# A head loop's turn re-ordered in 48 places, with the next group's first key products in its last eight, and a buffer of its own for the spread blocks' sum

## The chip, the cores and the metric

The kernel runs on one core of a Trainium2 chip. Its time is the device time of one execution in microseconds (us). Five engines work side by side, each through its own list of instructions in order: TensorE (PE, with its weight loads as PEld), VectorE (DVE), ScalarE (ACT), GpSimd (POOL) and SyncE (SP), which here only issues DMAs. They hand work to each other by semaphores.

## What is computed

The reference is a layer norm, followed by a gated delta-rule attention and a mixture of 16 experts on a part of the tokens, both added to the input. The part that this case is about, cut to what matters:

```python
q = silu(causal_dwconv(x @ Wq)); k = silu(causal_dwconv(x @ Wk)) * DK**-0.5; v = silu(causal_dwconv(x @ Wv))
alpha = sigmoid(x @ Wa + ba); beta = sigmoid(x @ Wb + bb)
def step(S, inps):
    qt, kt, vt, at, bt = inps
    Sk = einsum('bhvk,bhk->bhv', S, kt)
    err = Sk - vt
    S = at * S - bt * (err[..., None] * kt[:, :, None, :])
    ot = einsum('bhvk,bhk->bhv', S, qt)
    return S, ot
o = layernorm(scan(step)) * sigmoid(x @ Wg)      # per head
out = x + o @ Wo + experts(x)
```

There are 2 batches of 2048 tokens, 16 heads of width 128, and a model width of 512. All of it is float32; a projection is made as three fp32r products (high times high, high times low, low times high).

## The kernel before

Three stages follow each other: `prepare` (layer norm, experts, gates), `heads` (projections, convolution and scan for each head) and `project` (the output product). The change touches `heads` alone.

`heads` works on 32 batch-heads (`NH`), each in four groups of 512 tokens (g = 0 to 3), each group in four chunks of 128 tokens. One call of `turn` is one group's time step of a software pipeline. In the same turn an engine does work for groups at several ages:

- **Projection.** 48 products (12 for key, 12 query, 12 value, 12 gate; `project_some`) of the group that is four turns ahead of the scan, into three PSUM banks that take turns (`PJ_OF`). A bank is used again when its last reader has freed it (`PJ_FREED`): a convolution on DVE (`CONV_AT`, three multiply-adds for each of key, query and value) or the gate's tanh on ACT.
- **Inverse.** The scan over 128 tokens is solved with the inverse of a triangular matrix. PE makes the products `kT kT` (L_AT), DVE multiplies them into `LT` (LT_AT), ACT copies their diagonal blocks (DIAG_AT), POOL masks and sums them (LC_AT), SP stores the sum in DRAM twice and loads it back spread over all partitions as `Lb` (`spread`), POOL solves blocks of 16 in 15 steps of two instructions (`SOLVE_AT`), writes them back (T16P_AT), DVE transposes them into `Tnb` (T16_AT), and PE builds the larger blocks in two visits (`VISIT_AT`: visit 0 and visit 1).
- **The chain.** Twelve steps (`CHAIN`), three for each chunk, carry the state `S` on: k = 0, 3, 6, 9 is `S kT` on PE, answered by `R` on DVE; k = 1, 4, 7, 10 is `R TT` on PE, answered by `Wc` on ACT; k = 2, 5, 8, 11 is `Wc k_rows` on PE, answered by `S` on DVE.
- **Output.** The group's output is normalised by four DVE instructions `on` (ON_AT, one for each chunk), turned on PE (ON_TURN_AT), scaled on ACT (OT_AT) and gated on POOL (`oG`, OG_AT).
- **Weights of the next head.** Each of the four is cut once per head into a high part on ACT and a low part `w_lo` on POOL (`CUT_AT`: three in a turn with g = 3 and one in the next with g = 0).

The order on every engine is written out by hand: a turn has `STEPS` places, and each item's `_AT` number says in which place it stands. The number orders only instructions of one engine; nothing holds two engines at the same place. Before, there are 38 places, and PE sends its 48 products in one or two pieces at each.

Short names below: a "piece" is one of the 48 products, "V0" and "V1" are the visits, "k6" is chain step 6, "place 25" is s = 25.

```python
def wait(eng, sem, value):
    if isinstance(value, int) and value <= 0:
        return
    eng.wait_ge(sem, value)
```

Of the kernel before, what the change touches and what calls it, by code (L numbers as in the profile page):

```python
# [734 lines left out]
def heads(nc, bank, ident, pow_half, xT_hi_d, xT_lo_d, gates_d, base_d, oT_d, x_hi, x_lo, w_raw, w_cut, weights, taps, ln_w, ln_b,  # L735
# [10 lines left out]
    with ExitStack() as ctx:  # L746
# [760 lines left out]
        def _(pe):  # L1507
            def turn(pe, hh, g, n, chain, late, mid, inv, proj, ln, tile=None):
                at = counter(hh, g)
                par, cur = (g + 1) % 2, g % 2  # L1510
                sent = [0]

                def bank_waits(i):

                    back, user = PJ_FREED[g][i]
                    if user == 3:
                        wait(pe, tanh_done, at(1, 5 - back))
                    else:
                        wait(pe, conv_done, at(9, 4 - back, 3 * user + 3))
# [362 lines left out]
```

## Time and profile before

| | |
|---|---|
| median of three runs | 3578.73 us (3572.82 to 3580.15) |
| the profiled execution | 3573.76 us, its span 3568.4 us |
| PE busy | 3490.3 us, 98% of the span |
| DVE, ACT, POOL busy | 68%, 65%, 54% |
| granted TensorE clock, mean | 0.995 of full speed |
| stage `heads` | from about 418 us to about 3277 us of the span |
| first and last `LT` on DVE, one in each of 128 turns | 429.7 us and 3154.0 us |

PE's busy share is of little use by itself, since matmuls overlap: a piece is recorded with about 0.4 us but the next one starts 0.23 us after it. What a thing costs on PE is the distance from its start to the start of the next.

### The profile page before, as it was taken

The numbers are of one execution on the slowest core, as the hardware profiler recorded it, in microseconds if no ns is written. First come the engines' busy times: TensorE is split into PE (matmuls) and PEld (weight loads), VectorE is DVE, ScalarE is ACT, GpSimd is POOL, SyncE is SP. The second block draws the span as 40 slices with busy tenths as digits, with TensorE's granted clock in tenths as the row PEclk, the third lists the DMA queues.
The fourth block names the chain that finished last, engine by engine and source line by source line (L and its number), as shares of the span: only waits on it lengthen the run. The fifth ranks groups of instructions, "written<-read, shape, count | busy, mean of one in ns | idle before, by whom it ended". The sixth has DMA issues, their size and how long they took to land. (4 is left out here: it accounts for less than half of the span.)

```text
span 3568.4 us, 105534 instructions
## 1 busy us (share of the span) xinstructions
PE 3490.3 (98%) x32308; PEld 2912.9 (82%) x32308; DVE 2419.8 (68%) x5785; ACT 2303.3 (65%) x6448; POOL 1913.2 (54%) x4905
## 2 busy tenths in 40 slices
PE   8999989999999999999999999999999999999999
PEld 6787768888888888888888888888888888877887
DVE  6656557777777777777777777777777777753222
ACT  4443357777777777777777777777777777752111
POOL 3323256666666666666666666666666666653000
PEclk9999999999999999999999999999999999999999
DMA  8654523333333333333533333333333333444453
GB/s 307 217 197 164 172 60 76 77 83 87 82 79 77 77 81 82 77 79 76 146 102 84 79 77 78 76 77 85 79 76 79 76 77 81 107 156 127 142 148 111
DMA packets 427681, 375.89 MB, mean 105 GB/s; under 512 B 191984, under 2 KB 323056, under 8 KB 421248
## 3 DMA queue, kind: packets, MB, share of 16 engines
q1 hardware_dynamic: 424000, 362.46, 37.1%
q0 software_dynamic: 2080, 6.82, 0.5%
q8 instruction: 261, 4.28, 0.5%
q14 instruction: 284, 2.33, 0.2%
q10 hardware_dynamic: 1056, 0.02, 0.0%
HBM read 292.62 MB, written 76.58 MB: 103 GB/s over the span
## 5 line engine op out<-in xcount | busy, mean ns | idle before, releaser
L1329 DVE SCALAR_TENSOR_TENSOR conv<-bank,tap,conv 128x512 f32<-128x512 f32 x1152 | 862.3, 749 | 152.1 <-ACT conv L1465 123.9
L1155 POOL TENSOR_TENSOR prods<-Lb,Tc 128x60 f32<-128x60 f32 (+14 forms) x1920 | 480.1, 250 | 604.2 <-DMA Lb<-base_d 460.3
L1535 PE MATMUL bank<-hx_hi,w_hi 128*128 128x512 f32 x1536 | 664.3, 433 | 0.0
L1535 PE MATMUL bank<-hx_hi,w_lo 128*128 128x512 f32 x1536 | 645.3, 420 | 14.3 <-DVE Tnb L1291 11.5
L1535 PE MATMUL bank<-hx_lo,w_hi 128*128 128x512 f32 x1536 | 638.4, 416 | 0.0
L1162 POOL TENSOR_TENSOR Tc<-Tc,prods 128x56 f32<-128x56 f32 (+13 forms) x1792 | 460.1, 257 | 141.2 <-POOL prods L1155 1.7
L1446 ACT ACTIVATE Wc<-bank 128x128 f32<-128x128 f32 x512 | 140.9, 275 | 371.0 <-PE bank L1637 330.6
L1535 PEld LDWEIGHTS bank<-hx_hi,w_lo 128*128 128x128 f32 x1536 | 293.2, 191 | 50.9 <-DVE Tnb L1291 17.1
L1283 DVE SCALAR_TENSOR_TENSOR S<-S,gamma,bank 128x128 f32<-128x128 f32 x480 | 166.9, 348 | 234.3 <-PE bank L1648 221.0
L1535 PEld LDWEIGHTS bank<-hx_hi,w_hi 128*128 128x128 f32 x1536 | 292.4, 190 | 36.5
L1535 PEld LDWEIGHTS bank<-hx_lo,w_hi 128*128 128x128 f32 x1536 | 292.7, 191 | 29.5
L1465 ACT ACTIVATE conv<-bank,tap 128x512 f32<-128x512 f32 x384 | 264.4, 688 | 12.5
L1270 DVE SCALAR_TENSOR_TENSOR R<-bank,scale_c,v_rows 128x128 f32<-128x128 f32 x480 | 166.6, 347 | 125.4 <-PE bank L1624 125.4
L1637 PEld LDWEIGHTS bank<-R,TT 128*128 128x128 f32 x960 | 170.6, 188 | 85.3 <-DVE R L1270 39.4
L1139 POOL TENSOR_TENSOR w_lo<-w_raw,w_hi 128x512 fp32r<-128x512 f32 x152 | 194.9, 1283 | 74.1 <-ACT w_hi L1359 74.1
L1535 PE MATMUL bank<-x_hi,w_lo 128*128 128x512 f32 x512 | 212.0, 414 | 12.5 <-DVE Tnb L1291 8.1
L1535 PE MATMUL bank<-x_hi,w_hi 128*128 128x512 f32 x512 | 221.3, 432 | 1.0 <-PEq L151 1.0
L1648 PEld LDWEIGHTS bank<-Wc,k_rows 128*128 128x128 f32 x960 | 170.9, 189 | 60.8 <-ACT Wc L1446 35.8
L1624 PEld LDWEIGHTS bank<-S,kT 128*128 128x128 f32 x960 | 180.8, 189 | 41.8 <-DVE S L1283 0.7
L1535 PE MATMUL bank<-x_lo,w_hi 128*128 128x512 f32 x512 | 212.9, 416 | 0.0
L1397 ACT ACTIVATE same<-LT 32x128 f32<-32x128 f32 x512 | 157.1, 307 | 85.7 <-DVE LT L1348 72.7
L1648 PE MATMUL bank<-Wc,k_rows 128*128 128x128 f32 x960 | 197.4, 287 | 4.1
(211 smaller groups left out, 8855.4 us busy)
## 6 DMA issues: line engine op xcount, KB each, us to landing
Lb<-base_d SPq DMA_DIRECT2D x128, 512.0 KB, 4.7
gamma<-gamma_d SPq DMA_DIRECT2D x128, 258.0 KB, 3.5
alpha<-alpha_d SPq DMA_DIRECT2D x128, 256.0 KB, 3.2
oT_d<-oG SPq DMA_DIRECT2D x128, 256.0 KB, 4.4
gu_raw<-in_gate_up SPq DMA_DIRECT2D x16, 1408.0 KB, 6.3
o_raw<-oT_d SPq DMA_DIRECT2D x13, 1024.0 KB, 6.9
w_raw<-oT_d SPq DMA_DIRECT2D x12, 1024.0 KB, 7.0
dn_raw<-in_down SPq DMA_DIRECT2D x44, 256.0 KB, 6.7
```

The lines of the kernel that those rows point to most:

```text
L1139: pool.tensor_tensor(w_lo[:, i], w_raw[:, i], w_hi[:, i].bitcast(F32), ALU.subtract).then_inc(wlo_done, 1)
L1155: pool.tensor_tensor(prods[:, :, i + 1:], Lb[:, i, :, i + 1:], Tc[:, :, i:i + 1].to_broadcast([P, G, SB - 1 - i]), ALU.mult)\
L1162: pool.tensor_tensor(Tc[:, :, i + 1:], (sel if i == 0 else Tc)[:, :, i + 1:], prods[:, :, i + 1:], ALU.subtract).then_inc(solve_done, 1)
L1270: dve.scalar_tensor_tensor(out=R[:], in0=CO[:, 0:D], scalar=scale[:, cur, c:c + 1], in1=v_rows[:, cur, c], op0=ALU.mult, op1=ALU.add)\
L1283: dve.scalar_tensor_tensor(out=S[:], in0=S[:], scalar=gamma[:, cur, c, C:C + 1], in1=CO[:, 2 * D:3 * D], op0=ALU.mult, op1=ALU.add)\
L1329: dve.scalar_tensor_tensor(out=conv[i][:, to], in0=PJ[PJ_OF[g][i]][:], scalar=tap[:, i, j + 1:j + 2], in1=conv[i][:, to], op0=ALU.mult, op ...
L1397: act.activation(diag[quad(q)], LT[quad(q), g, :, quad(q)], ACT.Copy).then_inc(diag_done, 1)
L1465: act.activation(conv[i][:, KS - 1:], PJ[PJ_OF[g][i]][:], ACT.Copy, scale=tap[:, i, 0:1])\
L1535: last = pe.matmul(dst, a[:, i, k], b[:, k], start=(j == 0), stop=(j == 3 * KC - 1))
L1624: pe.matmul(CO[:, 0:D], kT[:, n % 6, chunk(c)], S[:], start=True, stop=True).then_inc(chain_done, 1)
L1637: pe.matmul(CO[:, D:2 * D], TT[:, n % 3, c], R[:], start=True, stop=True)\
L1648: pe.matmul(CO[:, 2 * D:3 * D], k_rows[:, cur, c], Wc[:], start=True, stop=True)\
```

## The change

The tables get new numbers for a turn of 48 places with exactly one piece in each. `LEAD = 8` shifts the pieces against the turn: a turn begins with piece 8 of its own group, and its last eight places take the first eight key pieces of the next group. The very first turn sends eight pieces ahead of its first place; the turns that make output tiles follow suit. `Lc`, the sum that SP stores, gets a buffer of its own instead of sharing `prods` with the solve, and the waits that guarded the shared one are changed; to make room, `Tn64` becomes the unused half of `MT`.

```diff
-STEPS = 38
+STEPS = 48
+LEAD = 8
-CHAIN = {0: 0, 7: 1, 8: 2, 11: 3, 15: 4, 18: 5, 19: 6, 22: 7, 23: 8, 26: 9, 28: 10, 36: 11}
+CHAIN = {0: 0, 6: 1, 9: 2, 14: 3, 18: 4, 20: 5, 22: 6, 25: 7, 27: 8, 33: 9, 40: 10, 43: 11}
-CUT_AT = {(3, 13): 0, (3, 21): 1, (3, 28): 2, (0, 19): 3}
+CUT_AT = {(3, 21): 0, (3, 30): 1, (3, 33): 2, (0, 14): 3}
...
-        Lc = prods
+        Lc = sb("Lc", [P, G, SB])
...
-        Tn64 = sb("Tn64", [2 * TB, G, 2 * TB])
+        Tn64 = MT[0:2 * TB]
...
-                sp.wait_ge(base_stored, at(32, d + 1))
+                stored = fixed(sp, at(32, d + 1), NH * GROUPS * 32)
+                solved = fixed(sp, at(SOLVE_PER, d), NH * GROUPS * SOLVE_PER)
+                sp.wait_ge(base_stored, stored)
+                wait(sp, solve_done, solved)
...
-                        wait(pool, solve_done, at(SOLVE_PER, 4))
+                        wait(pool, base_stored, at(32, 4))
...
-                        wait(act, masked, at(1, 4))
+                        wait(act, lc_done, at(1, 4))
...
-                sent = [0]
+                sent = [LEAD if proj and not (isinstance(hh, int) and hh < 0 and g == 0) or tile == 0 else 0]
...
+                        ahead, piece = divmod(sent[0], 3 * KC * NPROJ)
+                        i, j = divmod(piece, 3 * KC)
...
+                        hp, gp = (hh, g + ahead) if g + ahead < GROUPS else (hh + 1, 0)
+                        dst = PJ[PJ_OF[gp][i]][:]
...
+                if proj and isinstance(hh, int) and hh < 0 and g == 0:
+                    project_some(LEAD)
```

Other table entries that the prediction speaks of, before and after: L_AT 18 and 21, V0 20 and 33, V1 1 and 0, T16_AT 18 and 26, LT_AT 18 and 25, ON_AT 20 and 33, ON_TURN_AT 22 and 40, YB_AT 31 and 45, QG_AT (`q_gamma`) 24 and 22, OG_AT 25 and 34.

DVE, in the turn (0, 3) ahead of the loop, from the second chain `S` to the normalisation of the output. Before (the lines shown are numbered as in the kernel before):

```order
L1283 SCALAR_TENSOR_TENSOR S<-S,gamma,bank6 128x128 [waits s_done,chain_done]
L1291 STREAM_TRANSPOSE Tnb<-TTb 128x128 [waits tn_placed,mid_done,t16_done]
L1348 SCALAR_TENSOR_TENSOR LT<-bank5,decay 128x512 [waits late_done,diag_done,decay_done,l_done]
L1270 SCALAR_TENSOR_TENSOR R<-bank6,scale_c,v_rows 128x128 [waits chain_done]
L1315 TENSOR_SCALAR on<-o,hmv,hrstd 128x128 [waits o_turned,hrstd_done]
L1315 TENSOR_SCALAR on<-o,hmv,hrstd 128x128 x3
```

The same stretch of DVE's list after (lines from here on are three to five higher than before):

```order
L1286 SCALAR_TENSOR_TENSOR S<-S,gamma,bank6 128x128 [waits s_done,chain_done]
L1332 SCALAR_TENSOR_TENSOR conv1<-bank1,tap,conv1 128x512 [waits tap_done]
L1273 SCALAR_TENSOR_TENSOR R<-bank6,scale_c,v_rows 128x128 [waits chain_done]
L1332 SCALAR_TENSOR_TENSOR conv1<-bank1,tap,conv1 128x512 [waits conv_done]
L1351 SCALAR_TENSOR_TENSOR LT<-bank5,decay 128x512 [waits late_done,diag_done,decay_done,l_done]
L1294 STREAM_TRANSPOSE Tnb<-TTb 128x128 [waits tn_placed,mid_done,t16_done]
L1332 SCALAR_TENSOR_TENSOR conv1<-bank1,tap,conv1 128x512 [waits conv_done]
L1286 SCALAR_TENSOR_TENSOR S<-S,gamma,bank6 128x128 [waits s_done,chain_done]
L1273 SCALAR_TENSOR_TENSOR R<-bank6,scale_c,v_rows 128x128 [waits chain_done]
L1318 TENSOR_SCALAR on<-o,hmv,hrstd 128x128 [waits o_turned,hrstd_done]
L1318 TENSOR_SCALAR on<-o,hmv,hrstd 128x128 x3
```

`Tnb` of the last solve stood ahead of `LT` and stands behind it now; three convolutions of the query stand between the chain's answers.

POOL in a turn with g = 3, from the end of the solve on. Before:

```order
L1177 TENSOR_TENSOR TTb<-Tc,same_c 128x128 [waits placed,mid_done,solve_done]
L1183 TENSOR_TENSOR hrstd<-hveps,pow_half 128x4 [waits hveps_done]
L1139 TENSOR_TENSOR w_lo<-w_raw,w_hi 128x512 [waits whi_done]
L1167 TENSOR_TENSOR same<-same,same_c 128x128 [waits diag_done]
L1171 TENSOR_TENSOR prods<-same 128x64 [waits masked,solve_done]
L1139 TENSOR_TENSOR w_lo<-w_raw,w_hi 128x512 [waits whi_done]
L1189 TENSOR_TENSOR q_gamma<-qT,gamma 128x512 [waits chain_done,gamma_loaded0,silu_done]
L1197 TENSOR_TENSOR oG<-oT,gT 128x512 [waits gate_done,o_stored,oT_done]
L1139 TENSOR_TENSOR w_lo<-w_raw,w_hi 128x512 [waits whi_done]
```

After:

```order
L1180 TENSOR_TENSOR TTb<-Tc,same_c 128x128 [waits placed,mid_done,solve_done]
L1186 TENSOR_TENSOR hrstd<-hveps,pow_half 128x4 [waits hveps_done]
L1170 TENSOR_TENSOR same<-same,same_c 128x128 [waits diag_done]
L1174 TENSOR_TENSOR Lc<-same 128x64 [waits masked,base_stored]
L1142 TENSOR_TENSOR w_lo<-w_raw,w_hi 128x512 [waits whi_done]
L1192 TENSOR_TENSOR q_gamma<-qT,gamma 128x512 [waits chain_done,gamma_loaded0,silu_done]
L1142 TENSOR_TENSOR w_lo<-w_raw,w_hi 128x512 [waits whi_done] x2
```

The three weight cuts of the turn now stand all behind the sum, `q_gamma` between the first and the second, with nothing else in between; `oG` follows them.

PE in the loop, g = 1, from the products of `LT` to V0. Before (REGISTER_ALU rows are waits and counts of the sequencer):

```order
L1702 MATMUL bank5<-kT 128x128 x4
L1535 MATMUL bank0<-hx_hi1,w_hi 128x512
L1535 MATMUL bank0<-hx_lo1,w_hi 128x512
L1623 REGISTER_ALU
L1624 MATMUL bank6<-S,kT 128x128
L1562 REGISTER_ALU
L1566 REGISTER_ALU
L1535 MATMUL bank0<-hx_hi1,w_lo 128x512
L1589 MATMUL bank3<-Tnb,LT 32x32 x16
```

After, the end of the same way for g = 2:

```order
L1653 MATMUL bank6<-Wc,k_rows 128x128
L1659 MATMUL bank7<-Wc,AT 128x128
L87 REGISTER_ALU
L1540 MATMUL bank2<-hx_hi2,w_hi 128x512
L1540 MATMUL bank2<-hx_lo2,w_hi 128x512
L1540 MATMUL bank2<-hx_hi2,w_lo 128x512
L1540 MATMUL bank2<-hx_hi2,w_hi 128x512
L1540 MATMUL bank2<-hx_lo2,w_hi 128x512
L1567 REGISTER_ALU
L1571 REGISTER_ALU
L1540 MATMUL bank2<-hx_hi2,w_lo 128x512
L1594 MATMUL bank3<-Tnb,LT 32x32 x16
```

Between the products of `LT` and V0 stood three pieces and one chain matmul; now twelve pieces and five chain matmuls stand there, of which the last six pieces and two matmuls are shown.

## Rows read from the trace of the kernel before

**Rows 1.** The page: busy time of each engine, and its costliest DVE group.

```profile
PE 3490.3 (98%) x32308; PEld 2912.9 (82%) x32308; DVE 2419.8 (68%) x5785; ACT 2303.3 (65%) x6448; POOL 1913.2 (54%) x4905
...
L1329 DVE SCALAR_TENSOR_TENSOR conv<-bank,tap,conv 128x512 f32<-128x512 f32 x1152 | 862.3, 749 | 152.1 <-ACT conv L1465 123.9
```

**Rows 2.** Line L1348, one in each turn: count, durations, first and last start.

```profile
L1348 DVE SCALAR_TENSOR_TENSOR LT<-bank,decay x128: 652/685/694, 429.7 to 3154.0; 128x512 f32<-128x512 f32 x128
```

**Rows 3.** Timeline of PE, one turn: start, length, instruction, idle before.

```profile
1506.26 0.39 PE L1624 MATMUL bank<-S,kT 128*128 128x128 f32 x2
...
1507.09 0.49 PE L1637 MATMUL bank<-R,TT 128*128 128x128 f32 x2
...
1518.91 0.40 PE L1535 MATMUL bank<-hx_hi,w_lo 128*128 128x512 f32 x1
1519.14 0.40 PE L1535 MATMUL bank<-hx_hi,w_hi 128*128 128x512 f32 x1
...
1521.42 1.06 PE L1702 MATMUL bank<-kT 128*128 128x128 f32 x8
1522.23 0.47 PE L1535 MATMUL bank<-hx_hi,w_hi 128*128 128x512 f32 x1
...
1523.48 0.47 PE L1535 MATMUL bank<-hx_hi,w_lo 128*128 128x512 f32 x1 [0.32 <-DVE Tnb L1291]
1523.89 0.42 PE L1589 MATMUL bank<-Tnb,LT 32*32 32x32 f32 x28
...
1524.81 0.50 PE L1535 MATMUL bank<-hx_hi,w_hi 128*128 128x512 f32 x1
```

**Rows 4.** Waits from 1000 to 2500 us (70 turns): total us, times, longest.

```profile
POOL prods L1155 <- DMA Lb<-base_d: 243.0, 70, 5.0
...
PEld bank L1637 <- DVE R L1270: 21.4, 52, 0.4
```

**Rows 5.** Timeline of DVE, from 1500.5 and from 1520 us.

```profile
1501.13 0.66 DVE L1348 SCALAR_TENSOR_TENSOR LT<-bank,decay 128x512 f32<-128x512 f32 x1
...
1501.96 1.11 DVE L1315 TENSOR_SCALAR on<-o,hmv,hrstd 128x128 f32<-128x128 f32 x4
...
1522.83 0.31 DVE L1291 STREAM_TRANSPOSE Tnb<-TTb 128x128 f32<-128x128 f32 x1 [1.08 <-POOL TTb L1177]
1523.06 0.66 DVE L1348 SCALAR_TENSOR_TENSOR LT<-bank,decay 128x512 f32<-128x512 f32 x1
```

**Rows 6.** Timeline of POOL in the same turn.

```profile
1503.74 0.32 POOL L1171 TENSOR_TENSOR prods<-same 128x64 f32<-128x64 f32 x1
1504.02 1.19 POOL L1189 TENSOR_TENSOR q_gamma<-qT,gamma 128x512 f32<-128x512 f32 x1
...
1512.28 0.29 POOL L1155 TENSOR_TENSOR prods<-Lb,Tc 128x60 f32<-128x60 f32 x1 [4.98 <-DMA Lb<-base_d]
...
1522.33 0.46 POOL L1177 TENSOR_TENSOR TTb<-Tc,same_c 128x128 f32<-128x128 f32 x1 [0.22 <-POOL Tc L1162]
```

**Rows 7.** Timeline of SP's DMA queue in the same turn.

```profile
1507.30 0.57 SPq L980 DMA_DIRECT2D Lb<-base_d  x1
```

**Rows 8.** Timelines of DVE, POOL and PE, a turn of the last head, from 3178 us.

```profile
3178.88 3.04 DVE L1315 TENSOR_SCALAR on<-o,hmv,hrstd 128x128 f32<-128x128 f32 x4
...
3179.30 2.54 POOL L1139 TENSOR_TENSOR w_lo<-w_raw,w_hi 128x512 fp32r<-128x512 f32 x2 [3.73 <-ACT w_hi L1359]
...
3181.98 0.66 PE L1713 MATMUL bank<-ident,on 128*128 128x128 f32 x4 [0.83 <-DVE on L1315]
```

**Rows 9.** Timelines of DVE and POOL, a turn with g = 3, from 1178.5 us.

```profile
1179.71 2.25 DVE L1315 TENSOR_SCALAR on<-o,hmv,hrstd 128x128 f32<-128x128 f32 x4
...
1179.55 1.27 POOL L1139 TENSOR_TENSOR w_lo<-w_raw,w_hi 128x512 fp32r<-128x512 f32 x1
```

**Rows 10.** Timeline of DVE in the first turns, the lines of `LT`.

```profile
451.32 0.65 DVE L1348 SCALAR_TENSOR_TENSOR LT<-bank,decay 128x512 f32<-128x512 f32 x1
...
472.58 0.65 DVE L1348 SCALAR_TENSOR_TENSOR LT<-bank,decay 128x512 f32<-128x512 f32 x1
```

More of the change, by code:

```diff
@@ L48 @@
 NB = P // SB
-STEPS = 38
+STEPS = 48
 UNROLL = 3
+LEAD = 8
 PE_SLOT = 0
-CHAIN = {0: 0, 7: 1, 8: 2, 11: 3, 15: 4, 18: 5, 19: 6, 22: 7, 23: 8, 26: 9, 28: 10, 36: 11}
-PIECES = [len(range(-(-48 * i // STEPS), -(-48 * (i + 1) // STEPS))) for i in range(STEPS)]
+CHAIN = {0: 0, 6: 1, 9: 2, 14: 3, 18: 4, 20: 5, 22: 6, 25: 7, 27: 8, 33: 9, 40: 10, 43: 11}
 PJ_OF = [[0, 1, 2, 0], [1, 2, 0, 1], [2, 0, 1, 2], [0, 1, 2, 1]]
@@ L1510, in turn, with bank_waits @@
                 par, cur = (g + 1) % 2, g % 2
[L1511 to L1515 removed]
+                sent = [LEAD if proj and not (isinstance(hh, int) and hh < 0 and g == 0) or tile == 0 else 0]
+                def bank_waits(hp, gp, i):
+                    back, user = PJ_FREED[gp][i]
                     if user == 3:
[L1517 removed]
+                        wait(pe, tanh_done, counter(hp, gp)(1, 5 - back))
                     else:
[L1519 removed]
+                        wait(pe, conv_done, counter(hp, gp)(9, 4 - back, 3 * user + 3))
                 def project_some(pieces):
                     for _ in range(pieces):
[L1524 removed]
+                        ahead, piece = divmod(sent[0], 3 * KC * NPROJ)
+                        i, j = divmod(piece, 3 * KC)
                         k, part = divmod(j, 3)
                         sent[0] += 1
[L1527 removed]
+                        hp, gp = (hh, g + ahead) if g + ahead < GROUPS else (hh + 1, 0)
+                        dst = PJ[PJ_OF[gp][i]][:]
                         if j == 0:
[L1529 to L1534 removed]
+                            bank_waits(hp, gp, i)
+                            if i == 0 and not (isinstance(hp, int) and hp < 0 and gp == 0):
+                                pe.wait_ge(x_loaded[gp], (((hp + 1) >> 4) + 1) * 32)
+                            if not (isinstance(hp, int) and hp < 0):
+                                pe.wait_ge(wlo_done, hp * NPROJ + (i + 1))
+                        a, b = ((w_hi, x_hi[gp]), (w_hi, x_lo[gp]), (w_lo, x_hi[gp]))[part]
                         last = pe.matmul(dst, a[:, i, k], b[:, k], start=(j == 0), stop=(j == 3 * KC - 1))
@@ L1668, in turn @@
                         project_some(1)
-                    if tile is not None and tile < TILES:
+                    if tile is not None and tile < TILES and not (tile == 0 and s >= STEPS - LEAD):
                         out_some(1)
@@ L1672, in turn @@
                         visit(VISIT_AT[s])
-                    if proj:
-                        project_some(PIECES[s] - 1)
-                    if tile is not None and tile < TILES:
-                        out_some(PIECES[s] - 1)
                     if chain and s in CHAIN:
```

40 lines of the change are left out of this document (16 added, 24 removed).

## The prediction, made before the changed kernel ran

> **What bounds the kernel now.** I read the page first. PE is busy for 98% of the span, the others for 54 to 68% [rows 1]; since matmuls overlap, that does not say that PE never waits. So I took the turn. `LT` comes once in each of 128 turns, and the 127 distances between the first and the last make 21.45 us a turn [rows 2], 85.8 for a head's four. Against it stands what PE has to do in a turn, by the distance from start to start: a piece 0.23; four 128-column matmuls 0.81, and 0.08 more that shows in the piece behind them, so 0.223 each; a visit 0.92, and 0.12 to 0.2 around it [rows 3]. A turn has 48 pieces (11.1), 20 chain matmuls (4.5), eight for `kT kT` and `qT kT` (1.8), twelve transposes at half a matmul (1.3) and two visits (2.2): 20.9 us. At g = 0 two chain matmuls are missing (20.4), at g = 3 one (20.6). A head needs 82.8, so about 3.1 us of its 85.8 are waits: the most that an order can give back, 3.1 x 31 = 96 us.
>
> Then the waits. Two are local, on the chain. From k9 to k10 lie 0.83 us [rows 3] while PE has 0.69 of work there; `R` is what it waits for, as in 52 places of 70 turns [rows 4]. The third is V0, which waits for `Tnb` [rows 3]. Behind it is a ring. From `LT` at 1501.13 the work goes over ACT to the sum at 1503.74, over SP to the load at 1507.30, lands when the solve starts at 1512.28 (POOL had been idle for 4.98), takes 10.05 for the solve to `TTb` at 1522.33, and `Tnb` at 1522.83 stands ahead of the next `LT` on DVE, 1523.06 [rows 5 to 7]. That is 21.93 in this turn. It has no slack: whatever PE gains elsewhere, the ring takes back at V0.
>
> **The change, part by part.** Times are from a turn's start, by PE's distances above.
>
> The ring. `LT` now stands ahead of `Tnb` on DVE, so it no longer waits for the solve. The twelve pieces and five chain matmuls between L and V0 are 3.9 us, where three pieces and one matmul were. L starts at 10.1, `LT` at 12.6 (behind `R` of k6 and one convolution), the sum is done 2.9 later, the load has landed 7.7 after that (8.2 in the rows' turn [rows 6, 7]; a mean turn is 0.5 shorter than this one, and the spread is the part that varies), 10.1 for the solve, 0.5 to `Tnb` [rows 5, 6]: 12.9 in the next turn. DVE comes to `Tnb` at 13.2, V0 needs it at 14.6. That is 1.4 us of slack where there was none: the ring costs nothing now. At g = 0 the cut inside the solve adds 1.27 [rows 9], but the turn ahead of it is the long one below, so `Tnb` is ready at 12 there against 14.2: nothing either.
>
> The chain. k9 to k10 becomes seven pieces; the tightest is k6 to k7 with three pieces and a matmul, 0.92 against 0.83. k1, k4 and k7 have 0.9 until the next step; the answer of ACT takes no longer than that of DVE. I take no wait, and for handovers with under 0.1 to spare (k6 to k7, the key's SiLU ahead of L) one miss of 0.1 us in every second of the 96 turns with g = 0 to 2: +5 us in all, from the restart that a stalled weight load leaves.
>
> A new wait at g = 3. The gate's bank is freed there by the query's last convolution (`PJ_FREED`), and the gate begins at place 28, 13.5 us. On DVE that convolution stands behind `R` of k6 (11.7), a convolution, `LT` and `Tnb`, starts at 13.4 and ends at 14.2 with its 0.75 [rows 1]. +0.8 us, if nothing else held this turn.
>
> The larger one is `on`, also at g = 3. Four of these take 1.11 us together [rows 5]. With one `w_lo` on POOL beside the first they took 2.25: the first did not end before the cut [rows 9]. In the last head, two cuts back to back (2.54 for the pair) met the third and fourth: 3.04, and PE's transposes waited 0.83 for them [rows 8]. So each `on` that meets a long POOL instruction waits for its end, and POOL's next one goes ahead of the next `on`: one for one. Before, most of `on` met short work or none. Now the four meet the row sum, cut, `q_gamma`, cut, cut. By POOL: the sum ends at 15.6, cut to 16.8, `q_gamma` (1.19 [rows 6]) to 18.0, cut to 19.2, cut to 20.5. `on` starts at 17.5 (or 16.7 without the bank's wait); the first ends at 18.0, the second at 19.3, the third at 20.5, the fourth at 20.8. PE wants them at 18.35, place 40, and gets them at 20.85: 2.5 us, which contains the 0.8. Behind `on` stand three convolutions (0.78 apart), a memset and `Yb`, which ends at 23.5; V1 wants it at 23.1: 0.4 more. The turn is 20.6 + 2.5 + 0.4 = 23.6 with rounding. Both bounds are in the rows: with no lock it is 20.6 + 0.8 = 21.4, and with one cut's worth (as rows 9) 22.2.
>
> At g = 0, 1, 2 POOL's `q_gamma` ends at 16.7, when `on` starts: nothing. [...]
>
> The rest. `Lc` in its own buffer: its waits are met anyway, because POOL sums after the solve in its own order, and a load waits for stores as before: 0. SP's list keeps its order; `oG` comes late in the turn (19.9 to 21.2), but its store and what is queued behind it on SP (the loads of gamma and scale) wait for nothing sooner: 0. The eight pieces ahead only move work; their weights, cut at 16.8 in g = 3, are wanted at 17.7: 0. PE's sequencer has a few more waits among the pieces: 0 to 0.02 a turn. The first turns are bound by the ring alone (`LT` 21.26 apart with PE partly idle [rows 10]); without `Tnb` ahead of `LT` the solve (10.1), its write (0.5), the sum (0.8) and the spread (7.7) remain, 19.1: three turns, -6 us.
>
> **The sum.** A head after: 20.4 + 20.9 + 20.9 + 23.6 = 85.8, before 85.8; exactly, 85.73 against 85.84, over 31 heads -3. The first turns -6, small misses +5: -4 us on the profiled execution's 3573.8, so 3569.8. The median of the three runs lies 5.0 above that execution, and I keep the distance: 3574.8.
>
> **The rivals.**
> 1. *`on` gets through.* [...] Then g = 3 costs 21.4, a head 83.6, 2.2 less: -68, 3507. For it: four `on` overlap each other, 1.11 for four of 0.34 [rows 5]. Against: rows 8. Between the two, with one cut's worth, 22.2: -43, 3532.
> 2. *A new wait in every turn: slower.* On DVE `R` of k6 stands behind the query's first convolution, which needs ACT's copy at 10.7; it then leaves DVE free 0.24 us before `R` is due. If ACT is more than that behind its place, PE waits at k7, in each of 128 turns. At 0.5 us behind it costs 0.26 and the 0.1 of a restart: +46, 3621. It decides from 0.24 us on, and ACT's list up to there (key's SiLU, carried columns, copy) has no idle time in which to catch up.
> 3. *The ring still closes* through V0: the spread takes longer in the new places, where SP's stores and load meet other transfers. Nothing is lost up to 1.7 us more (12.9 to 14.6); from there each 0.1 costs 0.1 in 96 turns, so at 2.2 more +48, 3623. Against it: the rows' turn, with 8.2, is among the long ones.
> 4. *The order does not do what the table says* on the engines: excluded for the rows shown in the change above.
>
> **How the numbers follow.** Forecast as summed, 0.45: within it the two large terms are 96 recovered and 93 spent, each good to perhaps a tenth, so 3555 to 3592, with 0.15 faster, 0.2 within and 0.1 slower. Rival 1 in full 0.13, in part 0.16, both faster. Rivals 2 and 3 together 0.26: slower by the above, 0.02 of it within. Range: 3512 to 3612, which leaves out rival 1 in full and the far end of 2 and 3. About 0.2% (7 us) is what a measurement can tell from no change. Faster 0.44, same 0.22, slower 0.34.
>
> **What would show it.** Right: PE waits for `on` by about 2.5 us once per head and hardly at V0; `on` takes about 3.2 us for four at g = 3 and 1.1 elsewhere; `LT` 20.4 to 20.9 apart in three turns of four, 23.6 in the fourth; POOL's wait for the load of `Lb` shrinks from 3.5 us a turn to about 1 to 2. Wrong: a PE wait for `R` at k7, for `Tnb` at V0, or none for `on`.

## The result and the profile after

The changed kernel takes 3619.51 us (median of 4 runs, 3618.44 to 3620.94) against 3575.89 for the one before (4 runs): ratio 1.0121, 95% interval 1.0104 to 1.0139. It is 1.2% slower. The forecast was 3574.8 with a range of 3512 to 3612, so the time lies outside the range, and on the side that had a chance of 0.34.

The page after, then the line of `LT` (count, durations, first and last start); they answer to [rows 1, 2]:

```profile
PE 3461.0 (96%) x32308; PEld 2880.2 (80%) x32308; DVE 2395.4 (66%) x5785; ACT 2378.4 (66%) x6448; POOL 1917.1 (53%) x4905
...
L1332 DVE SCALAR_TENSOR_TENSOR conv<-bank,tap,conv 128x512 f32<-128x512 f32 x1152 | 855.9, 743 | 129.9 <-ACT conv L1468 119.5
```

```profile
L1351 DVE SCALAR_TENSOR_TENSOR LT<-bank,decay x128: 677/680/683, 428.8 to 3202.1; 128x512 f32<-128x512 f32 x128
```

The span is 3616.8 us. PE's share fell from 98% to 96%. From the first `LT` to the last lie 2773.3 us, before 2724.3: the 49 us that were lost are all in this stretch. I call it the stretch below; it compares runs of different hours better than medians do.

The waits from 1000 to 2500 us (total us, times, longest), answering to [rows 4]:

```profile
POOL prods L1158 <- DMA Lb<-base_d: 85.9, 51, 2.7
...
PE bank L1716 <- DVE on L1318: 29.4, 17, 1.8
...
PEld bank L1540 <- ACT MT L1421: 15.5, 51, 0.5
...
PE bank L1629 <- DVE S L1286: 13.1, 17, 0.9
PEld bank L1642 <- DVE R L1273: 12.5, 69, 0.2
...
PE bank L1540 <- DVE conv L1332: 8.3, 17, 0.5
```

POOL's wait for the spread blocks fell from 243.0 to 85.9 us, and no wait of PE for `Tnb` is left. In its place stand three waits that come 17 times each, once per head: for `on`, for `S` at L1629, for a convolution. One turn with g = 3 shows the first and the third. Timelines of POOL, DVE and PE (start, length, instruction, idle before), answering to [rows 8, 9]:

```profile
1537.81 0.32 POOL L1174 TENSOR_TENSOR Lc<-same 128x64 f32<-128x64 f32 x1
1538.09 1.27 POOL L1142 TENSOR_TENSOR w_lo<-w_raw,w_hi 128x512 fp32r<-128x512 f32 x1
1539.32 1.19 POOL L1192 TENSOR_TENSOR q_gamma<-qT,gamma 128x512 f32<-128x512 f32 x1
1540.48 2.51 POOL L1142 TENSOR_TENSOR w_lo<-w_raw,w_hi 128x512 fp32r<-128x512 f32 x2
```

```profile
1540.08 3.25 DVE L1318 TENSOR_SCALAR on<-o,hmv,hrstd 128x128 f32<-128x128 f32 x4
```

```profile
1536.76 0.50 PE L1540 MATMUL bank<-hx_hi,w_hi 128*128 128x512 f32 x1 [0.49 <-DVE conv L1332]
...
1543.56 0.63 PE L1716 MATMUL bank<-ident,on 128*128 128x128 f32 x4 [1.73 <-DVE on L1318]
```

The four `on` take 3.25 instead of 1.11 us: they end when POOL's chain of cut, `q_gamma`, cut, cut is through. The second wait is in the next turn, g = 0. Timelines of DVE, POOL and PE there:

```profile
1555.58 2.41 DVE L1342 TENSOR_TENSOR_SCAN decay<-alpha,diag_b 128x128 f32<-128x128 f32 x4
1557.91 0.32 DVE L1286 SCALAR_TENSOR_TENSOR S<-S,gamma,bank 128x128 f32<-128x128 f32 x1
```

```profile
1555.97 1.42 POOL L1142 TENSOR_TENSOR w_lo<-w_raw,w_hi 128x512 fp32r<-128x512 f32 x1
```

```profile
1558.28 0.49 PE L1629 MATMUL bank<-S,kT 128*128 128x128 f32 x2 [0.77 <-DVE S L1286]
```

Chain step k6 needs `S` of k5, which stands on DVE behind four scans `decay`. They take 2.41 us here and 1.37 in other turns, and the gate weights' cut lies on POOL at the same time. In the four turns of a head, V0 follows V0 after 21.09 us (into g = 1), 20.96 (g = 2), 21.82 (g = 3) and 23.87 (g = 0), together 87.74; before, they were 21.3 to 21.65, together 85.82 (means of 25 heads). From PE's distances start to start (the idle time in the rows above is only the larger part of each), the waits in the 87.74 are: `on` 1.90, k6 1.04, the gate's bank 0.75, a wait ahead of the V1 that follows g = 3 0.50, in all 4.19. Without them it is 83.6.

### The profile page after: what moved, and what is told of

It reads as the page before. It is cut to its first block and busy times, and to the rows that moved or that the text cites. A ratio compares the mean times of both kernels' runs of the same rounds, so it can differ in the third digit from the quotient of the medians.

```text
span 3616.8 us, 105912 instructions
## 1 busy us (share of the span) xinstructions
PE 3461.0 (96%) x32308; PEld 2880.2 (80%) x32308; DVE 2395.4 (66%) x5785; ACT 2378.4 (66%) x6448; POOL 1917.1 (53%) x4905
## 3 DMA queue, kind: packets, MB, share of 16 engines
q14 instruction: 285, 2.33, 0.2%
## 5 line engine op out<-in xcount | busy, mean ns | idle before, releaser
L1540 PE MATMUL bank<-hx_hi,w_hi 128*128 128x512 f32 x1536 | 662.5, 431 | 17.9 <-DVE conv L1332 17.9
L1540 PE MATMUL bank<-hx_lo,w_hi 128*128 128x512 f32 x1536 | 651.5, 424 | 0.0
L1540 PE MATMUL bank<-hx_hi,w_lo 128*128 128x512 f32 x1536 | 637.3, 415 | 11.5 <-DVE Tnb L1294 11.3
L1200 POOL TENSOR_TENSOR oG<-oT,gT 128x512 f32<-128x512 f32 x128 | 164.6, 1286 | 380.5 <-ACT oT L1491 380.5
L1540 PEld LDWEIGHTS bank<-hx_hi,w_lo 128*128 128x128 f32 x1536 | 292.3, 190 | 65.7 <-ACT MT L1421 27.4
L1540 PEld LDWEIGHTS bank<-hx_hi,w_hi 128*128 128x128 f32 x1536 | 292.2, 190 | 57.8 <-DVE conv L1332 24.3
L1540 PEld LDWEIGHTS bank<-hx_lo,w_hi 128*128 128x128 f32 x1536 | 292.9, 191 | 22.3
L1629 PE MATMUL bank<-S,kT 128*128 128x128 f32 x960 | 210.8, 301 | 23.2 <-DVE S L1286 23.2
L1540 PE MATMUL bank<-x_hi,w_lo 128*128 128x512 f32 x514 | 212.5, 413 | 11.7 <-issue 8.0
L1540 PE MATMUL bank<-x_hi,w_hi 128*128 128x512 f32 x515 | 221.8, 431 | 1.0 <-PEq L151 1.0
L1540 PE MATMUL bank<-x_lo,w_hi 128*128 128x512 f32 x515 | 218.0, 423 | 0.0
L1342 DVE TENSOR_TENSOR_SCAN decay<-alpha,diag_b 128x128 f32<-128x128 f32 x512 | 209.1, 469 | 7.0
L1629 PEld LDWEIGHTS bank<-S,kT 128*128 128x128 f32 x960 | 161.0, 189 | 63.8 <-DVE S L1286 33.3
L1318 DVE TENSOR_SCALAR on<-o,hmv,hrstd 128x128 f32<-128x128 f32 x512 | 208.3, 469 | 1.1 <-POOL hrstd L1186 1.1
```

Of the source, the lines that this page charges most:

```text
L1200: pool.tensor_tensor(oG[:], oT[:], gT[:, (n - 1) % 6], ALU.mult).then_inc(oG_done, 1)
L1318: dve.tensor_scalar(on[:, c], o[:, (g - 1) % 2, c], mv[:, c, 0:1], rstd[:, c:c + 1], ALU.subtract, ALU.mult).then_inc(on_done, 1)
L1342: last = dve.tensor_tensor_scan(decay[:, (n + 4) % 3, c, 1:1 + C], alpha[:, cur, chunk(c)], diag_b[:, c], 0.0, ALU.mult, ALU.add)
L1540: last = pe.matmul(dst, a[:, i, k], b[:, k], start=(j == 0), stop=(j == 3 * KC - 1))
L1629: pe.matmul(CO[:, 0:D], kT[:, n % 6, chunk(c)], S[:], start=True, stop=True).then_inc(chain_done, 1)
```

## The experiments

Ratios are to the kernel before on the same chip in the same hour, where its median was 3574.54 us for runs 1 to 4, 3562.26 for 5 to 8, 3574.20 for 9 to 12 and 3580.80 for 13 and 14. Between these sets I compare stretches and not ratios. The numbers are those of the labels.

**1 to 3, the cuts moved.** The first moves the gate's cut away from the scans; the second moves the other three away from `on`; the third does both.

```diff
-CUT_AT = {(3, 21): 0, (3, 30): 1, (3, 33): 2, (0, 14): 3}
+CUT_AT = {(3, 21): 0, (3, 30): 1, (3, 33): 2, (3, 47): 3}     # 1
+CUT_AT = {(3, 5): 0, (3, 32): 1, (3, 33): 2, (0, 14): 3}      # 2
+CUT_AT = {(3, 5): 0, (3, 32): 1, (3, 33): 2, (3, 47): 3}      # 3
-SOLVE_AT = {0: (0, 1), 1: (1, 6), 2: (6, 10), 5: (10, 11), ...
+SOLVE_AT = {0: (0, 1), 1: (1, 4), 6: (4, 11), ...             # 2, 3
+                        if s in (32, 33) and ln:               # 2, 3
+                            pool.wait_ge(on_done, at(4, 0))
```

> The changed kernel (3619.5 us) with one edit: the gate weights' cut (ACT's w_hi and POOL's w_lo) is taken from place 14 of the turn g=0 to place 47 of the turn g=3, where POOL does it after oG and ahead of the solve. Theory: in the changed kernel S of step k5 stands on DVE behind four decay scans, the second of which takes 1.14 us beside that cut and 0.40 elsewhere; so k6's matmul waits 1.02 us once a head. Without the cut beside them the scan goes back to 0.40 and some 0.75 of the 1.02 us go: 31 x 0.75 = 23, so 3596 us (3585 to 3602). Rival A: S is late only because the whole DVE row of that turn lags behind the on stall of the turn before: the scans get short, the wait stays, 3619 (3612 to 3624). Rival B: the cut delays the solve on its new place and V0 waits for Tnb: 3625 or more.

Measured: 3589.69 us, ratio 1.0044 (1.0029 to 1.0059), stretch 2743.6, that is 29.7 less. DVE in the same place of a head, and PE:

```profile
1456.70 1.37 DVE L1342 TENSOR_TENSOR_SCAN decay<-alpha,diag_b 128x128 f32<-128x128 f32 x4
1457.99 0.32 DVE L1286 SCALAR_TENSOR_TENSOR S<-S,gamma,bank 128x128 f32<-128x128 f32 x1
```

```profile
1458.49 0.38 PE L1629 MATMUL bank<-S,kT 128*128 128x128 f32 x2
```

The scans are back at 1.37, k6 waits for nothing, and the turn into g = 0 fell by 0.99. So the cut beside the scans is the cause, and more than I had split off: all of the 1.04, to rounding. One of the four scans takes 1.43 us beside the cut (at 1556.24 in the changed kernel), not the 1.14 that I expected from, and here all four take 0.40 to 0.43. `on` is as long as in the changed kernel (3.24), so Rival A, the lag behind it, is out.

> The changed kernel with the three cuts of the turn g=3 moved away from the four on: key between the steps i=3 and i=4 of the solve at g=3 (beside convolutions on DVE), query and value after the fourth on, for which POOL waits; the gate's cut stays beside the decay scans. Theory: on at g=3 goes from 3.48 us back to 1.36, and with it go the waits that stand on it per head: 1.89 for on at PE's transposes, 0.49 for the gate's bank, 0.55 for Yb at V1, together 2.9; DVE's row of g=0 is no longer late either, so k6's wait falls from 1.02 to about 0.3. 31 x 2.9 = 91 to 31 x 3.6 = 112 less: 3508 to 3529 us. Rival (the turn has another bound of 21.4 us close behind, as before, the ring through the spread and the solve): the head cannot go under 85.6, so 3553 us or more.

Measured: 3559.2 us, ratio 0.9957 (0.9942 to 0.9972), stretch 2715.2. The turn into g = 0 fell by 2.40 (the 1.90 of `on` and a half of k6, which waits in 13 of 25 heads now), but the turn into g = 3 rose from 21.82 to 22.18. The gain is 60 us and not 91 to 112; the bound of 85.6 a head in the rival is where this one lies, and only the next run tells that it isn't a bound.

> Both edits: the three cuts of g=3 moved as in the run before and the gate's cut moved to after oG. Theory: nothing of the two waits is left, a head takes 4 turns of the class without them, 4 x 20.96 = 83.8 against 87.74, so 3619.5 - 31 x 3.9 = 3498 us (3490 to 3510). If the k6 wait is due to DVE's lag alone, this run equals the one before. If the ring is what bounds, 3553 or more.

Measured: 3543.1 us, ratio 0.9916 (0.9898 to 0.9933), stretch 2699.6. DVE, POOL and PE at g = 3:

```profile
1432.30 1.11 DVE L1320 TENSOR_SCALAR on<-o,hmv,hrstd 128x128 f32<-128x128 f32 x4
1433.32 2.33 DVE L1334 SCALAR_TENSOR_TENSOR conv<-bank,tap,conv 128x512 f32<-128x512 f32 x3
```

```profile
1433.57 2.54 POOL L1142 TENSOR_TENSOR w_lo<-w_raw,w_hi 128x512 fp32r<-128x512 f32 x2 [2.40 <-DVE on L1320]
```

```profile
1428.99 0.50 PE L1542 MATMUL bank<-hx_hi,w_hi 128*128 128x512 f32 x1 [0.81 <-DVE conv L1334]
```

The turn into g = 0 is 20.94 now, 2.93 less than in the changed kernel: the 1.90 of `on` and the 1.04 of k6. The wait ahead of V1 stays (0.48) although `on` is in time, so `on` was not its cause; in this kernel MT32's copies on ACT end last before it. Two cuts run beside three convolutions, which keep their length (2.33 against 2.31 without cuts beside them). The forecast of 3498 is missed by 45 us. What spoils the sum is the gate's bank: the key's cut in the solve makes `TTb` late, `Tnb` waits for it and the convolution that frees the bank stands behind `Tnb`; the turn into g = 3 is 22.17.

**4, the cuts in halves**, nothing moved:

```diff
-                pool.tensor_tensor(w_lo[:, i], w_raw[:, i], ...).then_inc(wlo_done, 1)
+                for k in (slice(0, KC // 2), slice(KC // 2, KC)):
+                    last = pool.tensor_tensor(w_lo[:, i, k], w_raw[:, i, k], ...)
+                last.then_inc(wlo_done, 1)
```

> The changed kernel, nothing moved, but each w_lo is written by two POOL instructions of 256 columns instead of one of 512. It tests how DVE and POOL take turns. Theory (one for one: a DVE operation that is blocked gets in when the POOL operation running then ends, and the next POOL one comes after it): the second, third and fourth on are each blocked by half a cut, 0.65 to 0.75 instead of 1.33, 1.30 and 0.33, so the four on take 2.6 instead of 3.48 and the decay scans about 2.4 instead of 2.67: 0.9 to 1.2 us less per head, 3584 to 3592 us. Rival (POOL keeps what it holds until its run of ready work is done, whatever the size of its operations): the sum of the four on stays at 3.5 and the time at 3619 or above.

Measured: 3599.91 us, ratio 1.0078 (1.0060 to 1.0096), stretch 2758.2, 15.1 less than the changed kernel. DVE and POOL at g = 3:

```profile
1445.65 2.74 DVE L1320 TENSOR_SCALAR on<-o,hmv,hrstd 128x128 f32<-128x128 f32 x4
```

```profile
1445.04 1.20 POOL L1194 TENSOR_TENSOR q_gamma<-qT,gamma 128x512 f32<-128x512 f32 x1
1446.19 2.79 POOL L1143 TENSOR_TENSOR w_lo<-w_raw,w_hi 128x256 fp32r<-128x256 f32 x4
```

One for one holds: the four `on` last 0.67, 0.78, 0.76 and 0.76, where they were 0.52, 1.33, 1.30 and 0.33. The work beside them is the same, and the stall is shorter because four DVE instructions meet four short ones. The gain is half of what I expected: the first `on` takes 0.67, the fourth, which had been free, now meets a half too, and the scans, from which I had expected 0.27 us, take 2.37 together instead of 2.44.

**5, 7, 9, 10, the gate's bank and MT32**, all on top of 3. On DVE: 5 puts `Tnb` behind the query's last convolution, 7 puts that convolution ahead of `LT`, 9 orders convolution, `LT`, convolution, `Tnb`, `S`. 7 and 10 (on top of 9) also put MT32's copies ahead of `oT` on ACT.

```diff
-AT_AT, K_AT, T16_AT, TN64_AT, DECAY_AT, LT_AT = 14, 5, 26, 8, 19, 25
+AT_AT, K_AT, T16_AT, TN64_AT, DECAY_AT, LT_AT = 14, 5, 27, 8, 19, 25    # 5
+AT_AT, K_AT, T16_AT, TN64_AT, DECAY_AT, LT_AT = 14, 5, 26, 8, 19, 24    # 9, 10
-CONV_AT = {..., 20: (1, 0), 25: (1, 1), 26: (1, 2), ...}
+CONV_AT = {..., 20: (1, 0), 23: (1, 1), 24: (1, 2), ...}                # 7
+CONV_AT = {..., 20: (1, 0), 24: (1, 1), 25: (1, 2), ...}                # 9, 10
-MT32_AT, TT64_AT, MT64_AT, TT128_AT = 47, 4, 39, 5
+MT32_AT, TT64_AT, MT64_AT, TT128_AT = 41, 4, 39, 5                      # 7, 10
```

> The kernel with all four cuts moved (3543 us), with Tnb's transpose on DVE one place later, behind the query's last convolution. What is left above four turns of 20.96 us in that kernel is the turn into V0 of g=3, 22.17 us: the gate's first piece waits for the bank of that convolution, which stands behind Tnb, and Tnb waits for the solve's TTb. Theory (the gate's bank is bound by DVE's order): the convolution starts at 19.3 instead of 19.8 us after V0, the head falls by 0.5 us, 31 x 0.53 = 16, so 3527 us. Rival (it is the gate's tanh or weights that the piece waits for): 3543, no change. Second rival (V0 needs Tnb at once): 3550 or more.

Measured: 3540.32 us, ratio 0.9942 (0.9925 to 0.9958), stretch 2696.2. The turn into g = 3 fell by 0.55 as expected, but the other three rose by 0.15 to 0.30: at place 27 `Tnb` also stands behind `S` of k8, and V0 waited for it (16.4 us in 52 waits). Theory and second rival are both true in part.

> The kernel with all four cuts moved, and two more edits: the query's last two convolutions stand ahead of LT on DVE (places 23 and 24), so that the gate's bank is free when the piece comes; and the copies of MT32 stand ahead of oT on ACT (place 41 instead of 47), so that V1 does not wait for them. Theory: the turn into V0 of g=3 falls from 22.17 to 20.96, and 0.13 us goes from three turns of a head: 83.6 us a head against 85.16, 3543 - 31 x 1.6 = 3494 us (3488 to 3505). LT comes 0.7 us later, with 0.7 to 1.4 us of room before V0. Rival (the ring is close behind: LT 0.7 us later makes a turn of 21.3): 3525 or more, that is less than half of the gain.

Measured: 3565.66 us, ratio 1.0009 (0.9999 to 1.0018), stretch 2724.0: worse than 3. The time and the turns, all 21.4 to 21.7, fit the rival; its cause, the ring through the spread and `Tnb`, does not, since from 1000 to 2500 us DVE waits for `TTb` in one place, 0.4 us. DVE and POOL:

```profile
1436.47 1.52 DVE L1320 TENSOR_SCALAR on<-o,hmv,hrstd 128x128 f32<-128x128 f32 x4
```

```profile
1435.67 0.32 POOL L1174 TENSOR_TENSOR Lc<-same 128x64 f32<-128x64 f32 x1
1435.95 1.19 POOL L1192 TENSOR_TENSOR q_gamma<-qT,gamma 128x512 f32<-128x512 f32 x1
```

`LT` 0.7 us later makes POOL's sum and `q_gamma` later, and now `q_gamma` meets the first `on` in every turn (0.70 to 0.81 by group instead of 0.34). PE waits for it and, behind it, at V1. Two edits in one run: that this is `LT`'s doing and not MT32's is shown by run 10, which has MT32's edit too and no such stall.

> The kernel with all four cuts moved, with DVE's order of the turn's end changed to: the query's second convolution, LT, its third convolution, Tnb, S of step k8 (LT at place 24, convolutions at 24 and 25, Tnb at 26). The earlier try, with Tnb one place later, also put Tnb behind S of k8, and V0 then waited for Tnb (0.15 us in three turns, 0.30 in the fourth), which took back the 0.55 us that the gate's bank gave. Theory: now both are had; the third convolution starts at 19.3 us after V0, Tnb is ready at 20.3, which V0 still meets. The turn into V0 of g=3 is 21.6 us, the others stay at 20.96 to 21.08, 84.6 us a head: ratio to before 0.987 (0.985 to 0.989). Rival (V0 needs Tnb before 20.3 us): turns of 21.1 again and a ratio of 0.991 or more.

Measured: 3522.52 us, ratio 0.9859 (0.9843 to 0.9875), stretch 2679.0; turns 21.10, 20.97, 21.62, 20.94. As the theory says.

> The kernel before this one, and the copies of MT32 ahead of oT on ACT (place 41 instead of 47), for which V1's weights waited 0.13 us in three turns of a head. Theory: three to four times 0.1 to 0.13 us a head, 31 x 0.4 = 12 us: 0.3 to 0.4 points below the run before, 0.983. Rival (oT is then 0.95 us later, which holds PE's transposes of the next kind or ACT's vT): no gain or a loss.

Measured: 3512.98 us, ratio 0.9831 (0.9814 to 0.9847), stretch 2673.0. The gain over run 9 is real (the times of the two do not meet, and the stretch is 6.0 shorter) but lies in the turn into g = 0 alone (20.73 for 20.94), where the wait ahead of V1 goes from 0.48 to 0.27, not in the three turns that the theory named. This is the fastest kernel of the study, 1.7% under the one before and, by the stretch, 100 us under the changed one.

**11, MT32 alone** in the changed kernel (the last line of the diff above).

> The changed kernel (ratio 1.0121) with MT32's copies ahead of oT alone. Theory (V1's wait for MT32 in the turns without the on stall is a part of what the prediction had not counted): 0.13 us in three turns, 12 us, ratio 1.0087 (1.007 to 1.010). Rival (the wait is a margin that comes out somewhere else in the turn): 1.012.

Measured: 3613.41 us, ratio 1.0111 (1.0094 to 1.0127), stretch 2773.9 against 2773.3: nothing. The row `PEld bank L1540 <- ACT MT L1421` (15.5 us in 51 waits) is gone, and PE's distances around V1 are the same to 0.01: it was a wait of a weight load that ended before the matmul would have begun.

**8, the buffer undone** in the changed kernel (the changed waits of SP and ACT stay):

```diff
-        Lc = sb("Lc", [P, G, SB])
+        Lc = prods
-        Tn64 = MT[0:2 * TB]
+        Tn64 = sb("Tn64", [2 * TB, G, 2 * TB])
-                        wait(pool, base_stored, at(32, 4))
+                        wait(pool, solve_done, at(SOLVE_PER, 4))
```

> The changed kernel (3619.5 us) with the second part of the change undone alone: the spread blocks' sum lies again in the buffer of the solve's products, and Tn64 has its own. Theory (the prediction's step: the own buffer takes away waits that had long been fulfilled): 3619.5, within 6 us. Rival (the buffer is what let the spread start earlier; without it the solve waits longer for Lb): slower by the extra wait, 0.2 us or more a turn, 3645 or more.

Measured: 3614.94 us, ratio 1.0149 (1.0132 to 1.0166), stretch 2774.2 against 2773.3. The buffer is worth nothing.

**6, 13, 14, `Tnb` ahead of `LT` again.** 6 is on top of 3, 13 in the changed kernel, 14 in the kernel of 10.

```diff
-AT_AT, K_AT, T16_AT, TN64_AT, DECAY_AT, LT_AT = 14, 5, 26, 8, 19, 25
+AT_AT, K_AT, T16_AT, TN64_AT, DECAY_AT, LT_AT = 14, 5, 24, 8, 19, 25    # 6, 13
+AT_AT, K_AT, T16_AT, TN64_AT, DECAY_AT, LT_AT = 14, 5, 24, 8, 19, 24    # 14
+CONV_AT = {..., 20: (1, 0), 23: (1, 1), 26: (1, 2), ...}                # 13
+CONV_AT = {..., 20: (1, 0), 23: (1, 1), 25: (1, 2), ...}                # 14
```

> The kernel with all four cuts moved, with Tnb ahead of LT on DVE as in the kernel before. The prediction says that this order is what closed the ring LT, diagonal, sum, spread, solve, TTb, Tnb, LT. Theory: closed again, the ring takes 20.36 us from LT's end to TTb's end, then 0.31 Tnb and 0.66 LT, 21.33 us a turn, and 1.24 more in the turn whose solve carries the key's cut: 86.6 us a head against 85.16, so 3543 + 31 x 1.4 = 3587 us (3575 to 3595). Rival (the ring has room and only the gate's bank comes later by the 0.7 us that LT now stands between): 3563 us. Second rival (the order of the two does nothing): 3543.

Measured: 3691.51 us, ratio 1.0354 (1.0336 to 1.0372), stretch 2850.5: 151 us more than 3, where I had said 44. Place 24 lies ahead of the second convolution as well, so `Tnb`'s wait for the solve (102.0 us in 98 waits) held a convolution, `LT` and the one that frees the gate's bank. It shows that the ring closes, not what the swap is worth; hence the next two. A part of the 151 us is the clock: the mean granted clock over the stretch is 0.984 here and 0.996 in run 3 (see the last section).

> The changed kernel (ratio 1.0121) with one swap undone on DVE: the query's second convolution, Tnb, LT, its third convolution, so that Tnb stands directly ahead of LT as in the kernel before (the earlier run put it ahead of a convolution as well). Theory (the prediction's ring: LT, diagonal, sum, spread, solve, TTb, Tnb, LT): the way from LT's end to TTb's end is 20.36 us in the changed kernel, with 0.3 for Tnb and 0.66 for LT behind it 21.3 us a turn. The turns into V0 of g=1 and g=2, now 21.09 and 20.96, go to 21.3; the turn into V0 of g=3, 21.82, goes to 22.1, since LT keeps the gate's convolution 0.3 us longer; the turn with the on stall stays at 23.87. Together 0.9 us a head, 28 us, ratio 1.020 (1.017 to 1.023). Rival (the ring has room with Tnb ahead too, and the swap gives only the 0.3 us at the gate's bank): 0.3 us a head, 9 us, ratio 1.0147 or less.

Measured: 3658.85 us, ratio 1.0219 (1.0202 to 1.0236), stretch 2813.3, 40 more where the theory had 28. The ratio lies in the theory's range, but in good part by luck, for its parts are others: into g = 1 21.06 and into g = 2 21.18 instead of 21.3, into g = 3 22.35 instead of 22.1, into g = 0 24.21 instead of 23.87. That is 1.06 a head, of which I estimate 0.55 to be the clock (last section), and 8 us lie in the first turns (86.7 from the first to the fifth `LT`, 78.7 in the changed kernel). After the long turn the ring has room for one turn; the excess comes out at `on`, V1 and the gate's bank.

> The kernel with moved cuts, the new end of DVE's order and MT32 ahead of oT (ratio 0.983), with Tnb and then LT between the query's second and third convolution. No on stall leaves room to the ring here. Theory: 21.3 us in three turns, and in the turn whose solve carries the key's cut (1.24 us) up to 22.6; 86.6 us a head against 84.4, 68 us, ratio 1.002 (0.997 to 1.006), that is the whole gain is lost with this one swap. Rival (the ring has room): only the gate's bank, which the convolution now frees up to 1.2 us later in the turn into g=3: 85.6 us a head at most, 37 us, ratio 0.9935 or less.

Measured: 3605.21 us, ratio 1.0066 (1.0049 to 1.0082), stretch 2769.7 against 2673.0, 97 us more; a head takes 87.24 instead of the theory's 86.6. Against run 10, `Tnb` has moved ahead of two instructions, `LT` and the convolution that frees the gate's bank. Run 3 has the order convolution, `LT`, `Tnb`, convolution, from which this one differs by the swap of two DVE instructions and by MT32's copies: against it, it is 70 us. DVE and PE ahead of V0 of g = 3:

```profile
1453.70 0.31 DVE L1296 STREAM_TRANSPOSE Tnb<-TTb 128x128 f32<-128x128 f32 x1 [1.16 <-POOL TTb L1180]
1453.93 0.66 DVE L1353 SCALAR_TENSOR_TENSOR LT<-bank,decay 128x512 f32<-128x512 f32 x1
1454.51 0.74 DVE L1334 SCALAR_TENSOR_TENSOR conv<-bank,tap,conv 128x512 f32<-128x512 f32 x1
```

```profile
1455.31 0.50 PE L1542 MATMUL bank<-hx_hi,w_hi 128*128 128x512 f32 x1 [1.75 <-DVE conv L1334]
```

`Tnb` waits for the solve, and `LT` and the gate's bank wait behind it.

**12, the kernel before with its cuts moved**, so that none meets `on`:

```diff
-CUT_AT = {(3, 13): 0, (3, 21): 1, (3, 28): 2, (0, 19): 3}
+CUT_AT = {(3, 21): 0, (3, 26): 1, (3, 28): 2, (0, 19): 3}
```

> The kernel before with its key and query cuts moved within POOL's order of g=3 (key from behind the power of the solve's turn to behind the diagonal's sum, query from there to behind oG), so that the key's cut no longer meets the first on, which takes 1.01 us once a head instead of 0.34. Tells whether the old order would have had the same gain from moving cuts. Theory (the ring through the spread bounds it, and on is not in the ring): within 0.2%, 0.998 to 1.002. Rival (cuts beside on bound both kernels): 0.67 us a head less, 0.994.

Measured: 3575.76 us, ratio 1.0000 (0.9989 to 1.0012). From 600 to 2800 us the kernel before has 25 `on` above 0.5 us, here there is none, and nothing is gained. A blocked `on` was free in the old order: in these 2200 us PE waited for `on` in one place, 0.2 us.

## Why the prediction was wrong, point by point

**PE's work of a head: mis-sized by 0.8 us.** The sum took 82.8; the changed kernel without its waits has 83.6. The difference lies in the two visits, which I put at 2.2 a turn. PE around V0, answering to [rows 3]:

```profile
1538.03 0.40 PE L1540 MATMUL bank<-hx_hi,w_lo 128*128 128x512 f32 x1
1538.35 0.42 PE L1594 MATMUL bank<-Tnb,LT 32*32 32x32 f32 x28
...
1539.28 0.49 PE L1629 MATMUL bank<-S,kT 128*128 128x128 f32 x2
1539.52 0.48 PE L1540 MATMUL bank<-hx_hi,w_hi 128*128 128x512 f32 x1
1539.84 0.39 PE L1540 MATMUL bank<-hx_lo,w_hi 128*128 128x512 f32 x1
```

The piece ahead takes 0.32 instead of 0.23, the visit 0.93, and the chain matmul with the piece behind it 0.56 where 0.45 is usual: 1.12. V1 has 0.70 for the two pieces ahead of it and comes to 1.27. Together 2.4, in four turns 0.8 more, 25 us in 31 heads. This is read from the rows; no run isolates it.

**The ring: right.** With `LT` ahead of `Tnb` PE has no wait for `Tnb`, turns without other waits are 20.96 to 21.1, and POOL's wait for `Lb` is 1.2 us a turn (1 to 2 was said). Undone, the ring closes (13, 14). What the step did not say is where a closed ring shows: less at V0 than at `on` and at the gate's bank, since `LT` also releases `q_gamma`'s place in POOL's order and stands ahead of a convolution.

**The chain, "I take no wait": the step that failed.** k6 waits 1.04 us at g = 0, 32 us in all. I had costed the moved gate's cut as 1.27 us inside the solve and let the long turn hide it, that is on POOL's side alone, and looked for DVE's side of a cut only at g = 3. I had checked each chain step by the distance to its answer, without asking what stands between them on DVE: four scans ahead of `S`. Run 1 shows the cause: without the cut beside them the whole wait goes. The small misses that I added (+5) are not to be seen. Their 0.1 us is what the kernel before shows behind a weight load that had to wait: at 1507.09, where it had waited 0.41, the next matmul starts 0.32 after `R TT`, at 1519.84, where it had not, 0.22. So two terms of the sum failed, both on PE: this wait, put at nothing, and the visits, put 0.8 us a head too low.

**The gate's bank and `on`: right in kind, place and size.** 0.75 for the bank (0.8 said), 1.90 more at `on`, together 2.65 (2.5 said), 0.50 ahead of V1 (0.4 said). The last one is right in size only: I put it to `Yb` behind the late `on`, and it stays where `on` is in time (run 3), gives way by 0.2 when MT32 comes earlier there (run 10) and by nothing when it does so in the changed kernel (run 11), where `Yb` is as late. One for one, which rows 8 and 9 had only suggested, is shown by run 4. I had looked for it at `on`, where the kernel before has 1.20 us beside a cut (at 1179.71) and 0.34 without, and not at the scans: in the changed kernel one of the four takes 1.43 us beside the cut (at 1556.24) and the others 0.39 to 0.42. The convolutions keep their length: three take 2.33 us beside two cuts (run 3) and 2.31 without. Why they do, no run shows.

**The buffer: right. The first turns: right in the sum, by luck.** The buffer is worth 0 (run 8). From the first `LT` to the fifth it is 78.7 us, before 84.9: -6.2 against -6. But the forecast was three turns of 19.1, and the four distances are 12.81, 24.55, 20.05 and 21.27 (before 21.63, 21.25, 20.63 and 21.39): the second `LT` comes 8.8 us sooner, and the turn behind it gives 3.3 back.

**The sum again.** A head 87.74 instead of 85.73: 0.8 the visits, 1.04 k6, 0.15 `on` with the bank, 0.1 ahead of V1, to rounding, times 31 is 62 us. Against it stand the 5 of the misses, 4 of the median's distance (1.1 instead of 5.0), and some 4 in the first and last heads, where the stretch grew by 49 and not by 59 less 6. That makes 49; 45 were missed. The other 4 lie outside the profile: the profiled execution is longer than its span by 5.4 us before and by 1.6 after.

**The rivals.** Rival 1 (`on` gets through) and 3 (closed through V0) did not come. Rival 2 gave the right sign and nearly the time, 3621, by another place: there a wait at k7 in all turns, here one at k6 once per head. Its chance was priced for a new wait in every turn; a long one in one turn of four had no place in the list. The width was wrong as well: two terms of 96 and 93 us stood against each other, each taken as good to a tenth, and PE's floor had an uncertainty of its own that entered neither.

**What the new order was worth.** With the cuts out of the way of `on` and the scans it gives 0.8% (run 3), with DVE's and ACT's last places mended 1.7% (run 10); moving cuts in the old order gives nothing (run 12). So the gain was there, and the change's own table of cuts cost more than it.

## What to carry to other kernels

Place long POOL instructions by what DVE does at that moment. Here two cuts beside three convolutions cost nothing (2.33 us for 2.31). Beside `on` a cut cost about 1 us (1.33 for 0.34), beside the scans one cut cost 1.04 in all, and letting POOL wait for the end of `on` was cheaper than the collision (runs 2 and 3). When a step moves, look on every engine for what then lies beside it, not only for what it delays in its own list. And when an order removes the bound, list again what was hidden under it: a blocked `on` was free in the old order (run 12) and cost 1.90 us a head in the new one.
